# Where the second batch's first keys and values are projected: the handover between two attentions

## The reference

```python
xn = _layernorm(x, ln_scale, ln_bias)
q = (xn @ Wq).reshape(b, n, HEADS, d)          # 16 heads of 64
kv = xn @ Wkv
k, v = jnp.split(kv, 2, axis=-1)               # 4 groups of 64
q = _layernorm(q, qn_scale, qn_bias)
k = _layernorm(k, kn_scale, kn_bias)
dots = jnp.einsum('bghqd,bgkd->bghqk', qg, k) * scale
attn = jax.nn.softmax(dots, axis=-1)
out = jnp.einsum('bghqk,bgkd->bghqd', attn, v)
return out @ Wout
```

## Time and profile before

| | before |
|---|---|
| median of three runs | 804.23 us (803.65 to 804.3) |
| the profiled execution | 803.57 us, of which the span is 801.8 |
| PE busy | 770.0 us (96%) |
| DVE busy | 623.8 us (78%) |
| POOL busy | 591.7 us (74%) |
| ACT busy | 514.5 us (64%) |
| second batch's attention after the handover, first maximum scores | from 373.42 us |

### The profile page before, as it was taken

The page is one execution under the profiler, slowest core; times in us unless marked ns, Lnnn a source line. Parts: engine busy times, 40 slices in busy tenths (PEclk is TensorE's granted clock), DMA queues, the critical chain, the costliest instruction groups (busy, mean ns, idle before and its releaser), DMA issues.

```text
span 801.8 us, 21759 instructions
## 1 busy us (share of the span) xinstructions
PE 770.0 (96%) x8750; PEld 522.6 (65%) x8750; DVE 623.8 (78%) x1156; ACT 514.5 (64%) x957; POOL 591.7 (74%) x385
## 2 busy tenths in 40 slices
PE   5998999999999999999899999999999999999988
PEld 5665566666666666676555666666566656988877
DVE  6998788888888777366877788887888877679873
ACT  3875666766676776668656766676677666555522
POOL 2767777888888888946567888788888796455940
PEclk9999999999999999999999999999999999999999
DMA  7000000000000000000000000000000002200001
GB/s 187 5 2 1 2 3 2 2 3 2 2 2 3 2 3 2 2 1 2 1 2 2 2 2 2 2 2 3 3 2 2 3 2 55 58 1 2 1 1 52
DMA packets 50031, 8.57 MB, mean 11 GB/s; under 512 B 42631, under 2 KB 48523, under 8 KB 49931
## 3 DMA queue, kind: packets, MB, share of 16 engines
q1 hardware_dynamic: 49066, 7.05, 5.7%
q10 hardware_dynamic: 864, 0.13, 0.1%
HBM read 5.99 MB, written 1.05 MB: 9 GB/s over the span
## 4 chain that ended last, share of the span: by engine, by line
PE 80%; DVE 10%; issue 3%; ACT 2%; POOL 2%; DMA 1%; SPq 1%; DVEq 0%; ACTq 0%; POOLq 0%
PE psum L742 29%; PE psum L725 21%; PE psum L705 11%; PE psum L771 3%; DVE part L1299 2%; PE psum L591 2%; PE psum L758 2%; PE psum L593 1%; PE psum L592 1%; PE psum L1988 1%; PE psum L1911 1%; PE psum L1958 1%; PE psum L684 1%; ACT space L992 1%; PE psum L1945 1%
## 5 line engine op out<-in xcount | busy, mean ns | idle before, releaser
L560 POOL TENSOR_TENSOR space<-space 128x1024 f32<-128x1024 f32 x160 | 382.7, 2392 | 23.6 <-ACT space L992 5.5
L992 ACT ACTIVATE space<-psum 128x512 f32<-128x512 f32 x512 | 264.0, 604 | 38.2 <-PE psum L725 37.1
L742 PE MATMUL psum<-space,vb 128*32 128x256 f32 x4096 | 247.1, 382 | 2.1 <-ACT space L992 2.1
L1299 DVE TENSOR_REDUCE part<-psum 128x2 f32<-128x1024 f32 x150 | 183.3, 1222 | 32.3 <-PE psum L705 32.3
L742 PEld LDWEIGHTS psum<-space,vb 128*32 128x32 f32 x4096 | 120.9, 110 | 112.1 <-ACT space L992 37.7
L705 PE MATMUL psum<-kh,qh 64*128 64x512 f32 x512 | 117.0, 453 | 6.4 <-DVE part L1299 4.9
L565 POOL TENSOR_TENSOR space<-space 128x1024 f32<-128x1024 f32 x30 | 72.0, 2398 | 67.0 <-DVE space L1317 67.0
L1295 DVE TENSOR_REDUCE part<-psum 128x1 f32<-128x512 f32 x106 | 73.3, 691 | 49.2 <-PE psum L705 46.1
L725 PE MATMUL psum<-qh,kh 64*128 64x512 f32 x512 | 103.2, 396 | 0.1
L725 PE MATMUL psum<-qh,kl 64*128 64x512 f32 x512 | 101.7, 390 | 0.0
L725 PE MATMUL psum<-ql,kh 64*128 64x512 f32 x512 | 101.7, 391 | 0.0
(11 more groups left out here) (265 smaller groups left out, 1102.8 us busy)
## 6 DMA issues: line engine op xcount, KB each, us to landing
ql<-nmx SPq DMA_DIRECT2D x256, 0.5 KB, 2.0
wproj<-in_L_ffn_W SPq DMA_DIRECT2D x4, 256.0 KB, 2.7
out<-x SPq DMA_DIRECT2D x3, 256.0 KB, 2.0
x<-in_L_attn_x SPq DMA_DIRECT2D x2, 256.0 KB, 4.6
wproj<-in_L_attn_Wq SPq DMA_DIRECT2D x1, 512.0 KB, 6.8
x<-in_L_attn_x SPq DMA_DIRECT2D x1, 512.0 KB, 7.7
wout<-in_L_attn_Wout SPq DMA_DIRECT2D x8, 64.0 KB, 4.7
w1s<-in_L_ffn_W SPq DMA_DIRECT2D x2, 256.0 KB, 2.7
```

Source lines behind the costliest of these rows:

```text
L560: pool.tensor_tensor(to, pt[0] if u == 1 else to, pt[u], ALU.add)\
L742: last = pe.matmul(outp[quarter(h, hp), e * QB:(e + 1) * QB], vb[:, place(m)[1], kt, e * QUARTER:(e + 1) * QUARTER], pt[kt][:, h, hp * QB: ...
L992: act.activation(pt[kt][:, h, :], key_scores[kt % 2][h], ACT.Exp).then_inc(exp_made, 1)
L1299: dve.tensor_reduce(to[:, half, :], scores.rearrange("p (h k) -> p h k", h=2), AX_X, ALU.max, negate=True)\
```

## The change

Five edits, with no instruction added or taken away:

- The second batch's step 0 is projected into banks 0 and 1 instead of 2 and 3, and within the attention's loop: in phase 68 of the first batch, behind two value products and ahead of the last two. It waits for the rows and their high part (`xnt_made` 3, `x_high_made` 1).
- Only step 1 now waits for the last exponentials; step 2 waits for nothing any more, since its banks 2 and 3 are no longer those of step 0. PE projects step 2 behind the sums and ahead of the turning of step 0 (before: behind that turning).
- The turning of step 0, which writes banks 0 and 1, waits for the normal keys and the kept values of step 0 instead of for the maximum pass.
- POOL makes the twin of step 0 between the low part of the rows and that of the query weights (before: behind both).
- ACT keeps the values of step 0 ahead of the last `keep_out` (before: behind it).

```diff
--- before.py
+++ after.py
@@ -350,7 +350,7 @@
 
         def kv_at(b, s):
 
-            first = (2, 4, 6, 6) if b == 0 else (2, 4, 2, 4)
+            first = (2, 4, 6, 6) if b == 0 else (0, 4, 2, 4)
             return [banks(first[s] + i, 1) for i in range(2)]
 
         def key_sums(b, s):
@@ -533,9 +533,10 @@
                 if b:
                     pool.wait_ge(x_high_made, 1)
                     pool.tensor_tensor(c["row_low"][0][:, :], xnt[:, 1, :], c["row_high"][0][:, :].bitcast(F32), ALU.subtract).then_inc(x_low_made, 1)
+                    twin(b, 0)
                     pool.wait_ge(q_high_made, 1)
                     pool.tensor_tensor(c["q_low"][:, :], wproj[:, Q_AT:Q_AT + INNER], c["q_high"][:, :].bitcast(F32), ALU.subtract).then_inc(q_low_made, 1)
-                    for s in range(STEPS - 1):
+                    for s in range(1, STEPS - 1):
                         twin(b, s)
                     pool.wait_ge(u_high_made, 1)
                     pool.wait_ge(y_made, SLOTS)
@@ -595,11 +596,14 @@
             def keys_values(b, s):
 
                 n = STEPS * b + s
-                if b and s < 2:
+                if b and s == 0:
+                    pe.wait_ge(xnt_made, 3)
+                    pe.wait_ge(x_high_made, 1)
+                if b and s == 1:
                     pe.wait_ge(exp_made, 2 * TILES * SLOTS * b)
                 if n == 2:
                     pe.wait_ge(xnt_made, 2)
-                if s == 3 or (b and s == 2):
+                if s == 3:
                     before = n if b == 0 else n - 1
                     pe.wait_ge(kn_made, before)
                     pe.wait_ge(v_made, before)
@@ -616,7 +620,8 @@
                     pe.wait_ge(kh_made, n)
                     pe.wait_ge(kl_made, n)
                 elif b:
-                    pe.wait_ge(part_made, 8 * SLOTS * b)
+                    pe.wait_ge(kn_made, STEPS * b + 1)
+                    pe.wait_ge(v_made, STEPS * b + 1)
                 else:
                     pe.wait_ge(xnt_made, 2)
                 for g in range(GROUPS):
@@ -793,6 +798,8 @@
                     if scores_first:
                         m, k = divmod(ph, 4)
                         unit_scores(SLOTS * b + m, 2 * k + 1)
+                    if b == 0 and ph == 4 * SLOTS + LAG - 1:
+                        keys_values(1, 0)
                     m, k = divmod(ph - LAG - 5, 4)
                     if 0 <= m < SLOTS and k == 0 and SLOTS * b + m < LAST:
                         add_up(SLOTS * b + m)
@@ -868,13 +875,10 @@
             folded(0, 3)
             produce(0)
             attention(0, 4 * SLOTS + LAG + 1)
-            pe.wait_ge(xnt_made, 3)
-            pe.wait_ge(x_high_made, 1)
-            keys_values(1, 0)
             keys_values(1, 1)
             add_up(SLOTS - 1)
+            keys_values(1, 2)
             turn_keys(1, 0)
-            keys_values(1, 2)
             pe.wait_ge(w_float, 1)
             pe.wait_ge(out_kept, SLOTS)
             turn_w(0, 4, outp)
@@ -1126,8 +1130,8 @@
             act.wait_ge(pv_made, TILES * (SLOTS - 1) + 2)
             act.wait_ge(pool_added, ADDS * (SLOTS - 1) + 1)
             square_keys(1, 0)
+            keep_values(1, 0)
             keep_out(SLOTS - 1)
-            keep_values(1, 0)
             guess_keys(1, 0)
             square_keys(1, 1)
             keep_values(1, 1)
```

## The result

The changed kernel takes 806.37 us as the median of 22 executions (804.45 to 808.14), the kernel before 804.28 us (803.65 to 805.8). The ratio is 1.0022 with a 95% interval of 1.0016 to 1.0029: 1.8 us slower (the two medians alone differ by 2.1). The forecast was 804.6 us with a range of 802.9 to 805.6, and no change; the time lies outside the range.

The account below looks back on a forecast made before the run. TensorE was taken to bound the kernel, busy 770.0 of 801.8 us. A slip of 0.35 us on the basis of 804.23 gave 804.6 us, no change, range 802.9 to 805.6.

Parts of the forecast that it names:

- The order of the work: From the early projection near 337.9 to the folded projection near 362.55: forecast starts, with one PE wait of about 2.0 us.
- The size of the slip: DVE's sum of step 2, due at 350.48, was to slip by 0.35 us, to 350.83.
- the turning's delay: PE's turning of step 0, behind step 2's projection: 0.6 us later, at 347.5 instead of 346.90.
- The slack of 0.26 that DVE had: On DVE, between the low part of step 0 and the sum of step 2: 0.26 us absorbs part of the delay.
- The clock: TensorE's granted clock behind the new 2.0 us wait: assumed to stay at full speed, cost 0.
- this rival: Clock falls in PE's new wait at 349 to 351: up to 10.8 us longer, 815 us; chance 0.06.
- The basis: The starting time for the sum: 804.23 us, median of three runs, 0.66 above the profiled execution of 803.57.
- The filled gaps: PE's handover waits fill without replacement: first two or three, 803.15 or 802.85, chance 0.15; all five, 801.9, chance 0.06.
- the point that was named: Start of PE's turning of step 0: below 346.9 the filled-gaps rival wins, above it loses.
- The early projection: Step 0's projection among value products, 9.7 us of slack; rival that it isn't early: at most 804.2 us, chance 0.05.
- The slower case: Clock falls in PE's new 2.0 us wait: slower from 1.3 us of low-level path work, up to 10.8; chance 0.06.

Follow-up runs that it names:

- the third run of the changed kernel: The changed kernel with no edit, measured once more against the kernel before: 806.15 us, ratio 1.0021.
- the shifted one: The kernel before with six transposes of the identity added on TensorE's path at 373 us: 806.05 us, ratio 1.0014 to the kernel before.
- the changed kernel's fourth: The changed kernel with no edit, measured again against the kernel before: 806.02 us, ratio 1.0018.
- the first repeat: The changed kernel with no edit, measured again against the kernel before: 806.06 us, ratio 1.0012.

## Why the prediction was wrong, point by point

**The order of the work** came as forecast. PE took the early projection at 338.07 (forecast 337.9), ACT squared at 339.32 (339.2), guessed at 343.43 (343.1), POOL began the twin at 345.36 (345.0) with q_low behind it, the sums went at 344.66 without a wait (344.3), the turning of step 0 was late rather than early, and one wait of 2.03 us (2.0) stands before the turning of step 1 at 351.43 (351.05). Everything behind is only shifted, to the folded projection at 362.92 (362.55).

**The size of the slip** was too small by a half. The term is the turning's delay: forecast 0.6, measured 347.92-346.90 = 1.02, in the pair of profiles at full clock. A projection that stands alone between other work costs more than half of a pair: 338.07 to 340.00 is 1.93 and 342.74 to 344.66 is 1.92, where the double row gave 1.86; 32 value products in front of one take 1.86, not 1.8; and this execution was 0.08 late from the start (336.21). The slack of 0.26 that DVE had was right: the sum of step 2 slipped 351.20-350.48 = 0.72. At full clock the medians of the spans say 0.6, against 0.35.

**The clock** is the step that failed. I took 0 for it from one row: a wait of 2.03 us with the granted clock at 1.00. That was one execution. What the runs showed in its place is about 1.0 us for a mean execution (worked out below). In the profile of the third run of the changed kernel the same wait of the last stage is followed by a low stretch, at 771 to 774 us, and behind the handover's wait of 2.02 or 2.03 us two of five profiles of kernels with that wait show one (the one with the last stage's wait filled, and the changed kernel's fourth). The rule of the Trainium skill ("TensorE: Matmul & The Clock Gate", What's actually happening) that an idle array is gated down was the one to take seriously; the profiles above agree with it at the handover. It doesn't cover the stretch at 752.9 us in the first repeat, ahead of which PE had waited no more than 0.19 us since 745. The chance of 0.06 for this rival was far too small. Its price, "up to 10.8 us", was far too large: the low stretches of the changed kernel's profiles lasted 3.4 us and cost 1.5 us each (804.3 against 802.8).

**The basis.** The sum was made on an execution at full clock. The kernel before is one step down in 38 of 95 executions, with spans of 803.8 against 802.2 us. None of them was profiled; in the profile of the shifted one the episode is in the last stage. With three times given, 803.65 to 804.3, this was not to be seen. The range's upper end of 805.6 lies below the slowest execution of the kernel before (805.8), and only 1.0 us above the forecast.

**The sum as measured.** It is an estimate from the counts. At full clock +0.6. Steps down: 38 in 95 executions before, 34+2x12 = 58 in 54 after, so 0.40 and 1.07 for one execution; the difference of 0.67 at 1.5 us is +1.0. Together +1.6 us, 1.0020, against ratios of 1.0022, 1.0012, 1.0021 and 1.0018.

**The rivals.** The filled gaps did not come, since the turning started at 347.92 and not before 346.9, the point that was named. The early projection was early. The slower case came, though not in every execution.

**What stays open.** How often the handover's wait brings the clock down can't be read from one execution, since a single step may lie in either place. What calls the episodes of the last stage is not found. Of the seven profiles that have one, four have it begin at 770.5 to 770.9, 0.9 to 1.4 us behind the end of the last stage's 2.0 us wait, and three at 752.9 to 754.3, with no wait over 0.2 us in the 7 us ahead of it. No fewer were counted with the last stage's wait filled (6 of 12 executions against 8 of 22), and a shift of 0.7 us changed their number by less than 11 executions can show.

## What to carry to other kernels

When a reordering fills several short waits of TensorE, add up what it leaves: one wait of 2 us cost more here than the four of 0.3 to 0.8 us that it replaced, since it came with a later turning (0.6 us) and the granted clock could fall behind it (about 1 us for a mean execution). Work that the others wait for (here the turning of keys, with high part, low part and two copies behind it) goes ahead of work that nobody wants yet, even if that leaves a wait of 0.3 us. And before one execution's clock is taken as the kernel's, look at the clocks of many.

## What the runs showed of the hardware that was not expected

- The granted clock fell to half (1.2 GHz) behind a wait of 2.0 us at the handover, in some executions of the same program and not in others; the work behind it then took up to 1.9 times as long (3.50 us for 1.89) until the clock was back after 3.4 us, about 1.5 us in all. With a wait of 3.8 us it fell within the wait, the transposes were slow from their first, and it was back after 6.8 us; all 5 executions had a mean clock of 0.994 to 0.996.
- It also fell where TensorE was busy 3.60 of 3.60 us (752.7 to 756.3, a mean of 0.53), behind 24 matmuls of 40 columns.
- The first transfer of x let TensorE start at 6.27 us in one execution and at 7.49 in another, which is more than the whole effect of the order. Behind the last addition the span went on for 2.6 us in twelve profiles and for 3.7 and 3.9 in two.
